# An adapter, attention and quantised feed-forward block on one core: new step orders in the head loop, a fourth mask laid by ScalarE, and an adapter product in strips

## The chip, the cores and the metric

The kernel runs on one core of one Trainium2 chip. The metric is the device time of a launch in microseconds (us). The engines of the core work from their own instruction queues and meet at semaphores: TensorE (PE, with its weight loads as PEld), VectorE (DVE), ScalarE (ACT), GpSimd (POOL) and SyncE (SP), which here only issues transfers.

## What is computed

Eight sequences of 128 tokens with 512 features go through three stages, and each stage adds to x:

```python
h   = x @ W.T + b + 2 * (x @ A[id]) @ B[id]        # rank 16 adapter, one per sequence
q,k,v = dequant_matmul(h)                           # int4 weights, scales per 128 inputs: 4 row groups each
q,k = rope(q), rope(k)                              # 32 query heads, 8 key/value heads of 128
ctx = softmax(causal(q @ k.T / sqrt(128))) @ v
x   = x + dequant_matmul(ctx)                       # output product, 4 column groups per head
y   = (x @ B2[id2].T) @ A2[id2].T                   # second rank 16 adapter
y   = fake_quant_linear(layernorm(y), w1) ; gelu ; fake_quant_linear(y, w3)
out = x + y
```

Each of the 1,024 tokens meets only its own sequence in the attention. The weights w1 and w3 are rounded to 8 bits by row before use.

## The kernel before

All tokens stay in SBUF, features on partitions: `accT` holds x, and `h_hi` and `h_lo` hold the adapter's output as two fp32r parts whose sum is the fp32 value. The program has three parts: a prologue (adapter, weights of the feed-forward, first projections), a head loop of 8 groups (one key/value head and four query heads h = 0 to 3 each, the first and last group written out, six in a hardware loop), and the second adapter with the feed-forward as the tail.

**A step** is one `double_step` of TensorE (L1301, L1302): a 128x128 weight block against all 1,024 tokens of the upper and the lower part, four matmuls of 512 columns into a pair of PSUM banks. There are steps Q 0 to 3 (of a later head's query), K and V 0 to 3 (the next group's key and value, spread over the heads) and O 0 to 3 (the output product). A group has 40 steps. The table `PERIOD` gives their order, and since the three PSUM pairs are taken in turn, a step can start when the one three before it has been drained. ScalarE drains the steps Q0, K0 and V0 with their scale (L728); VectorE drains the others by a multiply and add into `raw_q`, `raw_k`, `raw_v` (L1018) or `accT` (L1032).

**Between the steps** each head has four kinds of fp32 block, in two halves f of four sequences that live in the PSUM banks `flow0` and `flow1`: `turn_probs` (L1410, transposes), `context` (L1418), `scores_ahead` (L1290, the next head's scores), and in head 3 `values_ahead` (L1295, transposes of the next group's v). A half's way through a head is: scores; `maxima` on VectorE (L983); `exps` on ScalarE (L685); `inverse` on VectorE (L1005); `normalise` on GpSimd (L538); `turn_probs`; `keep_turned` on ScalarE (L734); `context`; `keep_upper_context` on ScalarE (L751); `split_context` on VectorE (L1039). The causal mask of the scores is laid into the bank beforehand: by ScalarE (`seed_mask`, L746) for the scores that heads 0 to 2 make, and by a bf16 matmul of 512 columns (L1287) for those that head 3 makes.

**The rotation** of q and k needs each half of the head's 128 rows in the other's place. SyncE copies `raw_q` to `swap_q` by DMA (L408) once Q3 is drained, and `raw_k` to `swap_k` once K3 is. GpSimd then makes cosine part, sine part and sum in two halves each (L507, L519 for q; L523, L527, L533 for k).

**The prologue**: the adapter's first product (`lora_rows`, L1205) is made with the adapters of all eight sequences side by side for all tokens, a mask keeps each token's own 16 rows, and the second product (`linear_lora`, L1247) adds to the linear layer's bank (`linear`, L1242) with a contraction of 128. VectorE rounds the feed-forward weights (`quantise_weights`, L898 to L904). The first K and Q projections are made by halves of the tokens (`early_project`), and head 0 of the first group starts after `scores(1, 0)` and the transposes of v.

Every order is written out by hand in `body` for each engine; nothing is scheduled by a planner. A wait holds everything behind it on its engine.

## Time and profile before

| | us |
|---|---|
| median of 3 runs | 579.5 (579.35, 579.5, 583.7) |
| the profiled execution, its own time | 580.44 |
| its span, first to last instruction | 578.5 |
| granted TensorE clock over the span | 0.999 of full |

```profile
PE 549.6 (95%) x3065; PEld 429.3 (74%) x3069; DVE 494.2 (85%) x643; ACT 353.5 (61%) x923; POOL 399.9 (69%) x410
```

The row gives each engine's busy time, its share of the span and its instructions. The end of a matmul is modelled and contains its way through the array, so that one matmul's time overlaps the next one's: how fast TensorE goes is read from the distance between starts. A fp32 matmul stands in the trace as two instructions.

### The profile page before, as it was taken

What the parts mean: (1) busy time and instruction counts of PE and PEld (TensorE: products, weight loads), DVE (VectorE), ACT (ScalarE), POOL (GpSimd) and SP (SyncE); (2) the same over time, 40 slices, a digit from 0 to 9 for tenths busy, and PEclk for the clock granted to TensorE, in tenths of its full rate; (3) what the DMA queues carried; (4) which work ended last, traced back from release to release, by engine and by line L of the source; (5) the groups of instructions that cost most, each with busy time, mean ns of one, the idle gap of its engine ahead of it and who ended that gap; (6) DMA issues with size and microseconds to landing.
All of it is one profiled execution on the core that took longest, in us unless ns stands there. A gap on an engine that the chain in (4) does not pass through costs nothing.

```text
span 578.5 us, 10344 instructions
## 1 busy us (share of the span) xinstructions
PE 549.6 (95%) x3065; PEld 429.3 (74%) x3069; DVE 494.2 (85%) x643; ACT 353.5 (61%) x923; POOL 399.9 (69%) x410
## 2 busy tenths in 40 slices
PE   5999979999999999999999999999999999987885
PEld 4555557887888888878887888888878887875442
DVE  2894457998999899989998999899989998987897
ACT  2052447666766675666666766676666656765895
POOL 3003186699779977997799779977997799852064
...
GB/s 271 250 97 35 33 151 126 116 69 57 128 127 57 55 127 127 54 54 127 127 54 54 127 127 54 54 127 127 54 54 127 91 54 56 73 19 1 1 19 127
DMA packets 38171, 51.91 MB, mean 90 GB/s; under 512 B 12100, under 2 KB 20452, under 8 KB 38148
## 3 DMA queue, kind: packets, MB, share of 16 engines
...
q14 instruction: 12, 0.10, 0.1%
...
## 4 chain that ended last, share of the span: by engine, by line
PE 80%; DVE 10%; issue 3%; DMA 2%; ACT 2%; POOL 2%; SPq 0%; DVEq 0%; POOLq 0%; ACTq 0%
PE pair L1301 23%; PE pair L1302 22%; PE flow L1290 9%; PE flow L1418 8%; PE flow L1410 4%; PE pair L1242 4%; DVE y_max L1125 2%; DVE raw_v L1018 1%; PE flow L1295 1%; PE pair L1205 1%; PE flow L1242 1%; DVE raw_q L1018 1%; PE pair L1247 1%; DMA raw_q<-in_L_cond_W 1%; DVE rope_c L1137 1%
## 5 line engine op out<-in xcount | busy, mean ns | idle before, releaser
L1032 DVE SCALAR_TENSOR_TENSOR accT<-pair,so_now,accT 128x1024 f32<-128x1024 f32 x125 | 157.6, 1278 | 13.7 <-PE pair L1302 13.0
L1018 DVE SCALAR_TENSOR_TENSOR raw_q<-pair,sc_now,raw_q 128x1024 f32<-128x1024 f32 x90 | 115.5, 1283 | 3.5
L538 POOL TENSOR_TENSOR probs<-probs,rowinv 128x512 f32<-128x512 f32 x64 | 66.7, 1042 | 65.1 <-DVE rowinv L1005 65.0
L1301 PE MATMUL pair<-ctx_hi,wo 128*128 128x512 f32 x256 | 104.8, 409 | 2.7 <-issue 1.5
L685 ACT ACTIVATE probs<-flow,negmax 128x128 f32<-128x128 f32 x248 | 88.0, 370 | 31.0 <-DVE negmax L983 30.9
L1301 PE MATMUL pair<-h_hi,wq 128*128 128x512 f32 x240 | 100.0, 417 | 1.8 <-ACT raw_q L728 1.8
L1302 PE MATMUL pair<-ctx_lo,wo 128*128 128x512 f32 x256 | 100.2, 391 | 0.0
L1302 PE MATMUL pair<-h_lo,wq 128*128 128x512 f32 x240 | 94.1, 392 | 0.0
L507 POOL TENSOR_TENSOR rope_s<-swap_q,consts 128x512 f32<-128x512 f32 x62 | 80.1, 1291 | 10.2 <-DMA swap_q<-raw_q 10.2
L519 POOL TENSOR_TENSOR qT<-rope_c,rope_s 128x512 f32<-128x512 f32 x62 | 79.3, 1280 | 4.4
L507 POOL TENSOR_TENSOR rope_c<-raw_q,consts 128x512 f32<-128x512 f32 x62 | 78.7, 1290 | 0.0
L751 ACT ACTIVATE ctx_hi<-flow 128x512 fp32r<-128x512 f32 x64 | 38.4, 600 | 61.5 <-PE flow L1418 61.5
L1418 PEld LDWEIGHTS flow<-probsT,v_now 128*128 128x128 f32 x512 | 62.2, 191 | 13.7 <-ACT probsT L734 8.7
L1418 PE MATMUL flow<-probsT,v_now 128*128 128x128 f32 x512 | 69.9, 281 | 0.6 <-ACT probsT L734 0.4
L1290 PEld LDWEIGHTS flow<-kT,qT 128*128 128x128 f32 x496 | 65.0, 191 | 5.4 <-ACT flow L746 1.4
L1290 PE MATMUL flow<-kT,qT 128*128 128x128 f32 x496 | 65.4, 275 | 1.2 <-ACT flow L746 1.2
L1301 PEld LDWEIGHTS pair<-ctx_hi,wo 128*128 128x128 f32 x256 | 48.2, 188 | 13.5 <-DVE accT L1032 2.9
L1302 PEld LDWEIGHTS pair<-ctx_lo,wo 128*128 128x128 f32 x256 | 48.2, 188 | 8.5
L1301 PEld LDWEIGHTS pair<-h_hi,wq 128*128 128x128 f32 x240 | 45.2, 188 | 11.9 <-DVE accT L1032 2.2
L685 ACT ACTIVATION_READ_ACCUMULATOR probs<-flow,negmax 128x1 f32 x248 | 51.9, 209 | 0.0
L1039 DVE TENSOR_TENSOR ctx_lo<-flow,ctx_hi 128x512 fp32r<-128x512 f32 x64 | 43.8, 685 | 9.3 <-ACT ctx_hi L751 9.1
L1302 PEld LDWEIGHTS pair<-h_lo,wq 128*128 128x128 f32 x240 | 45.3, 189 | 7.2
...
## 6 DMA issues: line engine op xcount, KB each, us to landing
...
```

Source lines behind the costliest of these rows:

```text
L507: pool.tensor_tensor(per_seq(into[:, f, :]), per_seq(source[:, f, :]), on_each_seq(table), ALU.mult).then_inc(done, 1)
L519: pool.tensor_tensor(qT[:, (h + 1) % 2, half[f]], rope_c[:, f, :], rope_s[:, f, :], ALU.add).then_inc(q_roped, 1)
L538: pool.tensor_tensor(pr, pr, rowinv[:, f, :].unsqueeze(2).broadcast_to([P, HB, P]), ALU.mult).then_inc(probs_done, 1)
L685: e = act.activation(probs[:, 0, f, seq(b)], bank[:, seq(b)], ACT.Exp, bias=negmax[:, f, b:b + 1], accum_out=rowsum[:, f, b:b + 1])
L751: act.activation(ctx_hi[:, h % 2, half[f]], flow[f][:, :], ACT.Copy).then_inc(ctx_kept, 1)
L1018: dve.scalar_tensor_tensor(out=into, in0=flat(pair[pair_of(h, (kind, j), last)][:, :, :]), scalar=sc_now[:, scale_slot(kind, h), j:j + 1], ...
L1032: dve.scalar_tensor_tensor(out=a, in0=flat(pair[pair_of(h, (O, c), last)][:, :, :]), scalar=so_now[:, (h if c == 0 else h - 1) % 2, c:c + ...
L1039: dve.tensor_tensor(ctx_lo[:, h % 2, half[f]], flow[f][:, :], ctx_hi[:, h % 2, half[f]], ALU.subtract).then_inc(ctx_split, 1)
L1290: mm = pe.matmul(bank[:, seq(b)], qT[:, par, t], kT[:, t], start=False, stop=(b == HB - 1), skip_group_check=masked)
L1301: pe.matmul(into[:, f, :], w, upper[:, half[f]], start=True, stop=False)
L1302: mm = pe.matmul(into[:, f, :], w, lower[:, half[f]], start=False, stop=True)
L1418: mm = pe.matmul(flow[f][:, seq(b)], v_now[:, HB * f + b, :], probsT[:, f, seq(b)], start=(b == 0), stop=(b == HB - 1), skip_group_check=True)
```

## The change

It touches the prologue and the loop; the tail from the second adapter on is the same.

**The adapter in strips.** The rows of the adapters are placed so that a strip of 32 partitions holds those of sequences q and q + 4. The first product is 16 matmuls, each with 32 columns of weights and the 256 tokens of its two sequences, to 32 partitions of one bank; one mask by parity follows. The second product is 32 matmuls with a contraction of 32 rows and 128 tokens, in eight rounds of four; each round waits for the one before it.

```diff
-            def lora_rows(f):
+            def lora_rows():
 
                 for c in range(C):
-                    mm = pe.matmul(banks[4 + f], lA[:, c, :], accT[:, c, half[f]], start=(c == 0), stop=(c == C - 1))
-                mm.then_inc(u_done, 1)
+                    tokens = accT[:, c, :].rearrange("p (j b n) -> p b j n", j=2, b=HB)
+                    for q in range(HB):
+                        mm = pe.matmul(banks[4][STRIPS[q], 0:2 * P].rearrange("p (j n) -> p j n", j=2), lA[:, c, STRIPS[q]],
+                                       tokens[:, q, :, :], start=(c == 0), stop=(c == C - 1), skip_group_check=True)
+                        if c == C - 1:
+                            mm.then_inc(u_done, 1)
 
             for o in range(C):
                 turn_x(o, banks[o])
@@ -1239,12 +1506,17 @@
 
                 f, o = k // C, k % C
                 for c in range(C):
-                    pe.matmul(linear_bank(k), WT[:, c, seq(o)], accT[:, c, half[f]], start=(c == 0), stop=False)
-
-            def linear_lora(k):
-                f, o = k // C, k % C
-                pe.wait_ge(u_kept, f + 1)
-                pe.matmul(linear_bank(k), lB[:, seq(o)], uT[:, half[f]], start=False, stop=True).then_inc(lin_done, 1)
+                    pe.matmul(linear_bank(k), WT[:, c, seq(o)], accT[:, c, half[f]], start=(c == 0), stop=(c == C - 1))
+
+            def linear_lora(f):
+                pe.wait_ge(u_kept, 1)
+                for s in range(HB):
+                    wait(pe, strips_done, C * (HB * f + s))
+                    for o in range(C):
+                        q = (o + s) % HB
+                        mm = pe.matmul(linear_bank(C * f + o)[:, seq(q)], lB[STRIPS[q], seq(o)], uT[STRIPS[q], seq(f)],
+                                       start=False, stop=True, skip_group_check=True)
+                        mm.then_inc(strips_done, 1)
```

**Order of the prologue.** The second half of the linear layer is joined, ScalarE takes over two of VectorE's six passes over the feed-forward weights, GpSimd rotates in another order, and the first exponentials `exps(0, 0)` come ahead of the loop.

```diff
             pe.wait_ge(d_la, 16 * 2 * B)
-            lora_rows(0)
+            lora_rows()
             pe.wait_ge(scT_kept, 4)
             turn_weights(2)
-            lora_rows(1)
-            turn_weights(4)
-            for k in range(C):
-                linear_lora(k)
-            turn_weights(6)
+            linear_lora(0)
...
             linear(4)
-            linear_lora(4)
+            linear(5)
             pe.wait_ge(lo_made, C)
             pe.wait_ge(wk_made, 1)
             early_project(K, 0, 0)
-            linear(5)
-            linear_lora(5)
+            turn_weights(4)
+            turn_weights(6)
             pe.wait_ge(wq_made, 1)
             early_project(Q, 1, 0)
             pe.wait_ge(ffT_kept, 4)
             linear(6)
-            linear_lora(6)
             linear(7)
-            linear_lora(7)
+            linear_lora(1)
+            early_project(K, 2, 1)
+            early_project(Q, 3, 1)
             pe.wait_ge(diag_made, 2 * C)
-            pe.wait_ge(lo_made, C + 2)
             for m in range(2):
                 pe.matmul(banks[4 + m], ones, diag[:, m, :], start=True, stop=True).then_inc(ffrow_done, 1)
-            pe.wait_ge(lo_made, 2 * C)
-            early_project(K, 2, 1)
-            early_project(Q, 3, 1)
             pe.wait_ge(k_roped, 1)
             pe.wait_ge(q_roped, 1)
             scores(0, 0, score_bank(0, False))
...
+            def round_weights(k):
+                m, c = k // C, k % C
+                act.wait_ge(ff_top, k + 1)
+                act.activation(w_nat[k], w_nat[k], ACT.Identity, bias=magic, scale=ff_inv[:, m, c:c + 1]).then_inc(ff_rounded, 1)
+
+            def take_weights(k):
+                act.wait_ge(ff_clipped, k + 1)
+                act.activation(w_rounded[k], w_nat[k], ACT.Copy, bias=-HALF_MAGIC).then_inc(ffq_made, 1)
...
             early_wide(V, 5, V_PAIRS[0])
+            exps(0, 0, score_bank(0, False))
```

**The loop.** `PERIOD` and the bodies of all engines have new orders. SyncE issues the weight loads of a head ahead of the swaps, except for the output weights, which come behind. ScalarE lays the mask for the scores of head 3 too (`SEEDED`), the second half of it at the start of the next head 0.

```diff
-        PERIOD = [[(Q, 0), (O, 1), (Q, 1), (Q, 2), (Q, 3), (K, 0), (O, 2), (O, 3), (K, 1), (O, 0)],
-                  [(Q, 0), (O, 1), (Q, 1), (Q, 2), (Q, 3), (K, 2), (O, 2), (O, 3), (K, 3), (O, 0)],
-                  [(Q, 0), (O, 1), (Q, 1), (Q, 2), (Q, 3), (V, 0), (V, 1), (O, 2), (O, 3), (V, 2), (O, 0)],
-                  [(Q, 0), (O, 1), (Q, 1), (Q, 2), (Q, 3), (V, 3), (O, 2), (O, 3), (O, 0)]]
+        PERIOD = [[(Q, 0), (O, 1), (Q, 1), (Q, 2), (K, 0), (Q, 3), (O, 2), (K, 1), (O, 3), (O, 0)],
+                  [(Q, 0), (O, 1), (Q, 1), (Q, 2), (K, 2), (O, 2), (Q, 3), (O, 3), (K, 3), (O, 0)],
+                  [(Q, 0), (O, 1), (V, 0), (Q, 1), (Q, 2), (V, 1), (O, 2), (Q, 3), (O, 3), (V, 2), (O, 0)],
+                  [(Q, 0), (O, 1), (Q, 1), (V, 3), (Q, 2), (Q, 3), (O, 2), (O, 3), (O, 0)]]
...
-        SEEDED = REP - 1
+        SEEDED = REP
...
-                    if h < 2 or not last:
-                        load_output(g + h // 2, (h + 2) % REP)
                     if h == 1 and not last:
                         load_q(g + 1)
+                        if loads:
+                            load_kv(g + 2)
                     if present(h, (Q, 3), first, last):
                         sp.wait_ge(dve_drained, drains_by(g, h, (Q, 3), first, last))
                         wait(sp, q_sin, 2 * n + 2)
                         swap(swap_q, raw_q, swapped_q)
+                    if h < 2 or not last:
+                        load_output(g + h // 2, (h + 2) % REP)
                     if h == 1 and not last:
-                        if loads:
...
+                    elif h == 2:
+                        q_cosine(0)
+                        q_cosine(1)
+                        q_sine(0)
+                        q_add(0)
+                        normalise(0)
+                        k_cosine(0)
+                        normalise(1)
+                        q_sine(1)
+                        q_add(1)
+                        k_sine(0)
+                        k_cosine(1)
+                        query_scale()
+                        output_scale()
+                    else:
+                        q_cosine(0)
+                        q_cosine(1)
+                        q_sine(0)
+                        k_sine(1)
+                        normalise(0)
+                        q_sine(1)
+                        normalise(1)
+                        output_scale()
+                        q_add(0)
+                        k_add(0)
+                        q_add(1)
+                        k_add(1)
+                        query_scale()
```

The bodies of head 3 on TensorE and VectorE, as they are now:

```diff
+                    else:
+                        project(Q, 0)
+                        output(1)
+                        project(Q, 1)
                         project(V, 3)
-                    context(1)
...
+                        turn_probs(0)
+                        project(Q, 2)
+                        context(0)
+                        turn_probs(1)
+                        project(Q, 3)
+                        context(1)
+                        values_ahead(0)
                         output(2)
...
                         output(3)
...
+                        scores_ahead(0)
+                        values_ahead(1)
+                        output(0)
                         scores_ahead(1)
```

ScalarE's mask, and the start of head 0:

```diff
+                        if h == 3:
+                            act.wait_ge(v_kept, 2 * (g + 1) + f + 1)
+                        else:
+                            act.wait_ge(ctx_split, 2 * n + f + 1)
                         act.activation(per_seq(flow[f][:, :]), on_each_seq(tri), ACT.Copy).then_inc(mask_seeded, 1)
...
+                    def seed_mask_before():
+
+                        if not first and SEEDED == REP:
+                            act.wait_ge(v_kept, 2 * g + 2)
+                            act.activation(per_seq(flow[1][:, :]), on_each_seq(tri), ACT.Copy).then_inc(mask_seeded, 1)
...
+                    elif h == 0:
+                        round_kv()
+                        round_output()
+                        round_query()
+                        keep_values_before()
+                        seed_mask_before()
+                        exps_now(0)
+                        drain_query()
+                        exps_now(1)
```

Three places in the order of the instructions. First TensorE in the prologue, from the last part of the first half's linear layer to the first K projection. Before:

```order
L1242 MATMUL pair<-accT,WT 128x512 x12
L1218 MATMUL flow<-consts,rope_c 128x128
L1221 MATMUL flow<-consts,rope_c 128x32 x2
L1225 MATMUL flow<-consts,rope_c 128x32 x4
L1235 MATMUL flow<-ident_b,w_q 128x128 x8
L1205 MATMUL pair<-accT,qT 128x512 x4
L1235 MATMUL flow<-ident_b,w_q 128x128 x8
L1205 MATMUL pair<-accT,qT 128x512 x4
L1235 MATMUL flow<-ident_b,y_qT 128x128 x8
L1247 MATMUL pair<-kT,qT 128x512 x4
L1235 MATMUL flow<-ident_b,y_qT 128x128 x8
L1242 MATMUL pair<-accT,WT 128x512 x4
```

And now (L1509 is the linear layer, L1502 the transposes of rounded weights, L1470 and L1517 the two products of the adapter):

```order
L1509 MATMUL pair<-accT,WT 128x512 x12
L1485 MATMUL flow<-consts,rope_c 128x128
L1488 MATMUL flow<-consts,rope_c 128x32 x2
L1492 MATMUL flow<-consts,rope_c 128x32 x4
L1502 MATMUL flow<-ident_b,w_q 128x128 x8
L1470 MATMUL pair<-accT,qT 32x256 x16
L1502 MATMUL flow<-ident_b,w_q 128x128 x8
L1517 MATMUL pair<-raw_v,qT 128x128 x16
L1509 MATMUL pair<-accT,WT 128x512 x8
```

Eight matmuls of the first product became 16 of a quarter of the size each way, the second product of the first half is one block of 16, and two blocks of transposes moved behind the first K projection.

Second, ScalarE from the end of head 3 to the first exponentials of head 0, in the hardware loop, whose first instruction is the branch. Before:

```order
L751 ACTIVATE ctx_hi<-flow 128x512
L739 ACTIVATE v_now<-flow 128x512
L319 UNCONDITIONAL_BRANCH
L319 ISA
L755 ISA
L660 ACTIVATE wo<-wo_i 128x512
L668 ISA
L660 ACTIVATE wq<-wq_i 128x512
L738 REGISTER_ALU
L739 ACTIVATE v_now<-flow 128x512
L683 ISA
L685 ACTIVATE probs,rowsum<-flow,negmax 128x128 x4
```

And now (L849 and L860 lay the mask, L747 turns integer weights into fp32r):

```order
L839 ACTIVATE v_now<-flow 128x512
L849 ACTIVATE flow<-consts 128x512
L326 UNCONDITIONAL_BRANCH
L326 ISA
L747 ACTIVATE wkv<-wkv_i 128x512
L868 ISA
L870 ISA
L747 ACTIVATE wo<-wo_i 128x512
L755 ISA
L747 ACTIVATE wq<-wq_i 128x512
L838 REGISTER_ALU
L839 ACTIVATE v_now<-flow 128x512
```

The mask of flow0 is laid behind the copy of the first half's values; ahead of the copy of the second half's stands one more conversion of weights, and behind it the second mask.

Third, GpSimd in head 2 of the hardware loop, from the first cosine on. Before (L507 cosine and sine of q, L538 normalise, L519 sum of q, L523 and L527 cosine and sine of k):

```order
L507 TENSOR_TENSOR rope_s<-swap_q,consts 128x512
L538 TENSOR_TENSOR probs<-probs,rowinv 128x512 x2
L551 REGISTER_ALU
L552 ISA
L552 COPY so_now<-so_cols 128x4
L519 TENSOR_TENSOR qT<-rope_c,rope_s 128x512
L507 TENSOR_TENSOR rope_s<-swap_q,consts 128x512
L519 TENSOR_TENSOR qT<-rope_c,rope_s 128x512
L522 ISA
L523 TENSOR_TENSOR raw_k<-raw_k,consts 128x512
L527 TENSOR_TENSOR swap_k<-swap_k,consts 128x512
L523 TENSOR_TENSOR raw_k<-raw_k,consts 128x512
```

And now (L521, L552, L533, L537 and L541 in the same roles):

```order
L521 TENSOR_TENSOR rope_s<-swap_q,consts 128x512
L533 TENSOR_TENSOR qT<-rope_c,rope_s 128x512
L552 TENSOR_TENSOR probs<-probs,rowinv 128x512
L536 ISA
L537 TENSOR_TENSOR raw_k<-raw_k,consts 128x512
L552 TENSOR_TENSOR probs<-probs,rowinv 128x512
L521 TENSOR_TENSOR rope_s<-swap_q,consts 128x512
L533 TENSOR_TENSOR qT<-rope_c,rope_s 128x512
L541 TENSOR_TENSOR swap_k<-swap_k,consts 128x512
L537 TENSOR_TENSOR raw_k<-raw_k,consts 128x512
```

The first sum of q moved ahead of the first normalise, and the first cosine of k, with its wait for the DMA of `swap_k`, between the two normalises.

## Rows read from the trace of the kernel before

**Rows 1.** The page: shares of the chain that ended last, by engine.
```profile
PE 80%; DVE 10%; issue 3%; DMA 2%; ACT 2%; POOL 2%; SPq 0%; DVEq 0%; POOLq 0%; ACTq 0%
```
**Rows 2.** Stretches (start:end length), busy PE PEld DVE ACT POOL: first head; heads of group 2.
```profile
82.53:97.37 14.84, 11.86 (x71) 9.43 (x70) 7.61 (x10) 12.65 (x38) 11.35 (x12) 1.00 0.29 72
197.82:211.70 13.88, 13.88 (x84) 11.76 (x82) 11.59 (x14) 9.57 (x26) 12.27 (x13) 1.00 0.26 63
211.70:225.40 13.70, 13.70 (x83) 11.76 (x82) 13.34 (x16) 8.63 (x25) 9.86 (x10) 1.00 0.52 147
225.40:240.14 14.74, 14.74 (x88) 12.51 (x86) 14.21 (x16) 10.12 (x30) 11.32 (x13) 1.00 0.44 107
240.14:254.88 14.74, 14.41 (x89) 11.78 (x88) 13.71 (x16) 9.03 (x28) 13.73 (x15) 1.00 0.22 53
```
**Rows 3.** Timeline of TensorE: start, duration, line, operation, count [idle before <-releaser].
```profile
196.78 0.39 PE L1287 MATMUL flow<-tri_b,ident_b 128*128 128x512 bf16 x1
197.01 1.05 PE L1290 MATMUL flow<-kT,qT 128*128 128x128 f32 x8
...
201.59 0.60 PE L1410 MATMUL flow<-consts,probs 128*128 128x128 f32 x4
201.95 0.48 PE L1301 MATMUL pair<-h_hi,wq 128*128 128x512 f32 x1
202.26 0.39 PE L1302 MATMUL pair<-h_lo,wq 128*128 128x512 f32 x1
202.49 0.40 PE L1301 MATMUL pair<-h_hi,wq 128*128 128x512 f32 x1
...
233.89 1.05 PE L1418 MATMUL flow<-probsT,v_now 128*128 128x128 f32 x8
234.70 0.48 PE L1301 MATMUL pair<-ctx_hi,wo 128*128 128x512 f32 x1
...
249.90 0.66 PE L1295 MATMUL flow<-consts,raw_v 128*128 128x128 f32 x4 [0.33 <-DVE raw_v L1018]
```
**Rows 4.** Timeline of VectorE, group 3: two adds to accT, three drains of one Q.
```profile
264.85 2.47 DVE L1032 SCALAR_TENSOR_TENSOR accT<-pair,so_now,accT 128x1024 f32<-128x1024 f32 x2
...
272.75 3.92 DVE L1018 SCALAR_TENSOR_TENSOR raw_q<-pair,sc_now,raw_q 128x1024 f32<-128x1024 f32 x3
```
**Rows 5.** Timeline of ScalarE, group 3: one mask laid into a flow bank.
```profile
264.11 0.60 ACT L746 ACTIVATE flow<-consts 128x512 f32<-128x512 f32 x1
```
**Rows 6.** The tile swap_k in groups 1 to 6: its DMA.
```profile
DMA to landing us min/median/max: 3.3/3.6/4.0
```
**Rows 7.** Timeline of GpSimd, group 2: the first normalise of head 2.
```profile
228.08 1.04 POOL L538 TENSOR_TENSOR probs<-probs,rowinv 128x512 f32<-128x512 f32 x1 [2.64 <-DVE rowinv L1005]
```
**Rows 8.** Timeline of TensorE: adapter products whole, and the tail's product in strips.
```profile
29.41 3.65 PE L1205 MATMUL pair<-accT,qT 128*128 128x512 f32 x8
...
37.28 3.65 PE L1247 MATMUL pair<-kT,qT 128*128 128x512 f32 x8
...
531.55 1.78 PE L1501 MATMUL flow<-accT,low_bT 128*32 128x256 f32 x24
```
**Rows 9.** Timeline, end of the prologue: second K half, its swap, the scores.
```profile
65.38 2.46 DVE L967 SCALAR_TENSOR_TENSOR raw_k<-pair,sc_now,raw_k 128x512 f32<-128x512 f32 x3 [1.58 <-ACT raw_k L674]
...
72.59 1.29 POOL L476 TENSOR_TENSOR raw_k<-raw_k,consts 128x512 f32<-128x512 f32 x1 [11.33 <-DMA swap_k<-raw_k]
...
80.47 0.38 PE L1287 MATMUL flow<-tri_b,ident_b 128*128 128x512 bf16 x1 [1.41 <-POOL qT L481]
```
**Rows 10.** Timeline, head 0 of the first group: TensorE's longest wait.
```profile
86.45 0.50 PE L1301 MATMUL pair<-h_hi,wq 128*128 128x512 f32 x1 [1.75 <-ACT raw_q L728]
```
**Rows 11.** Timeline, last group: the last swap of q, and the scores it leads to.
```profile
503.83 1.10 SPq L408 DMA_DIRECT2D swap_q<-raw_q  x2
...
508.78 1.29 POOL L507 TENSOR_TENSOR rope_s<-swap_q,consts 128x512 f32<-128x512 f32 x1 [1.28 <-DMA swap_q<-raw_q]
...
517.20 1.05 PE L1290 MATMUL pair<-kT,qT 128*128 128x128 f32 x8
```

587 lines of the change are left out of this document (406 added, 181 removed).

## The prediction

> **What bounds the kernel now.** I read the shares of the chain first: TensorE holds 80% of it [rows 1], so a gain must come out of TensorE's own time or out of its waits. Then the stretches by head: the four heads of a loop group take 13.88 + 13.70 + 14.74 + 14.74 = 57.06 us, TensorE is called busy for nearly all of it, and VectorE for 11.59 + 13.34 + 14.21 + 13.71 = 52.85 [rows 2]. Busy does not tell how full TensorE is, so the timeline comes next, by distances between starts [rows 3]. A matmul of 512 columns follows another after 0.23 us (202.26 to 202.49), 0.91 to 0.92 for a step of four. The first one behind an fp32 block takes 0.31 (201.95 to 202.26), 0.08 more. A `turn_probs` takes 0.36 (201.59 to 201.95), a `context` 0.81 (233.89 to 234.70); scores have the same eight instructions of 1.05 us and I take 0.81; a mask matmul takes 0.23 (196.78 to 197.01).
>
> A group is then 40 steps x 0.91 = 36.4, 8 x (0.36 + 0.81 + 0.81) = 15.8, two value transposes 0.7 and two mask matmuls 0.5, together 53.4. It has 21 places where an fp32 block ends and a step follows: 21 x 0.08 = 1.7. That makes 55.1 of 57.06: 1.9 us of a group are waits, the largest the value transposes behind VectorE's last drain of v (0.33 alone [rows 3]). VectorE has 4.2 us of room in a group.
>
> **The loop, part by part.** *Fewer block ends.* The new order sets blocks side by side (both turns in head 0, both contexts in heads 0 and 2, both scores in heads 0 to 2). I count 15 ends instead of 21: 6 x 0.08 = 0.5 us less. *Fourth mask by ScalarE.* Two mask matmuls go, 0.5 us; ScalarE lays two more masks at 0.60 [rows 5] and is busy 9.57 + 8.63 + 10.12 + 9.03 = 37.35 of 57 us in those heads [rows 2], so the work fits; its place is the question, below. *VectorE's order.* Adds to accT follow each other after 1.19 (2.47 less a last one of 1.28), the three drains of one Q after 1.32 (3.92 less 1.28, halved), since each waits for its predecessor's result [rows 4]. The new order separates five of eight such neighbours: 5 x 0.13 = 0.6 us less. The ideal sums are now TensorE 54.1 and VectorE 52.2.
>
> *New and kept waits.* I laid the four heads out with these durations, starting TensorE's step as soon as its pair is drained and each engine in its written order. Head 0: the second turn waits for exponentials 1 and normalise 1, 0.3. Head 1: context 1 waits for ScalarE's copy, 0.1. Head 2: V1 and context 1 wait for ScalarE, 0.3 together. Head 3: context 0 and 1, 0.3, and scores 1: ScalarE must copy the second half's values (after three conversions of weights) and only then lay the mask, about 0.6 + 0.6 behind the end of the transposes, against 1.0 for the O0 step between them, so 0.5. With rounding of starts that makes 1.7 us, the group 55.8, and I take **1.2 us less a group**. The bounds: all waits gone, 57.06 - 54.1 = 2.9 less; none of it gained, 0. I take a value nearer to the waits of the layout, since VectorE stands in it without a pause in heads 1 and 2 and passes on every delay. Six groups of the hardware loop: -7.2. Heads 1 to 3 of the first group: -0.9.
>
> *SyncE's order.* The query and key/value loads now go ahead of head 1's swap of q, and stand well before it; the output loads go behind it, two heads ahead of their use. A swap of k takes 3.3 to 4.0 us to land [rows 6]. K3's drain moves later, to about 0.4 us into head 2, so it lands at about 4.2. Behind it GpSimd now holds the second normalise of head 2, which must end by 7.9, when TensorE turns it: cosine 1.3 and normalise 1.0 make it 6.5. Nothing, but see the rivals. GpSimd used to idle 2.64 us ahead of head 2's first normalise [rows 7]; the sum of q now fills that.
>
> **The prologue.** Each adapter product takes 3.49 us for a half (3.65 less the tail of the last [rows 8]), 14.0 in all. In strips: the tail's product of the same shape issues 24 instructions in 1.78, so 8 in about 0.5 to 0.6 [rows 8]; the first product has 32, 2.2 us instead of 7.0. The second has 64 of half the columns in eight rounds of 8, and each round waits for the last to end: at least the issue of a round and one latency, 0.5 to 0.6 a round, 4.4 instead of 7.0. TensorE loses 7.4 us of work. Not all reaches the loop: the split of the second half into upper and lower part used to lie beside the linear steps and now comes behind all of it (passes of 128x512 on ScalarE and VectorE in turn, about 0.6 each as the mask in [rows 5]: I let the first projection of that half start 1.5 us behind the last strip). Followed on, the drain of the second K half ends at 61 to 62 instead of 67.84 [rows 9], its swap lands 4.7 us later as before (67.84 to 72.59 [rows 9]), GpSimd has made both cosines in that time, so the scores that waited until 80.47 for its sum could start at 71 to 72; TensorE's and VectorE's own queue of wide Q and V steps comes to them at 73 to 74 and ends some 6 us earlier than before. **-5.8**, bounds: -2 if strips and split eat the rest, -8 if TensorE's queue has no waits of its own.
>
> The Trainium skill ("TensorE: Matmul & The Clock Gate", the cost: per-tile semaphore tail) says that increments of concurrent tiles' semaphores serialize, 25 + 4.7 ns a tile + 26.3 ns an increment. By that, eight rounds of four increments would cost 8 x 0.15 = 1.2 us more than nothing, an estimate from that page; the tail's strips above have an increment on each matmul and their 1.78 contains it.
>
> **First head.** It took 14.84 us [rows 2]; its seven steps and blocks need 7 x 0.91 + 4.0 + 0.4 = 10.8. The largest wait is 1.75 for ScalarE, which made the first exponentials before it drained Q0 [rows 10]. Those are now made beside the wide steps. A wait on the second half's exponentials stays (about 1.1), and the two contexts, whose copies feed the masks, stay in line. I take 12.9: **-2.0**, bounds 0 and -3.5.
>
> **Last group.** Its head 2 is short and waits for head 3's query: swap issued at 503.83, landed 508.78, scores 517.20 [rows 11]. Q3 now stands behind both turns and a context in head 1 (0.36 + 1.0 + 0.81 + 0.36 = 2.5 us later on TensorE; VectorE, then behind two more operations, ends it some 1.4 later). Heads 0 and 1 give back 0.2. **+1.2**, bounds -0.5 and +3.
>
> **Sum.** -5.8 - 2.0 - 0.9 - 7.2 + 1.2 = -14.7 on the profiled execution's 580.44: 565.7. The median of the runs shown is 579.5, 0.9 below it: **565**.
>
> **Rivals.**
> 1. *VectorE sets the pace of the loop, or its lag turns into waits at S1 and the masks, and a group stays at 56.6 or more.* For: 52.2 of work in a group, no pause in two heads. Against: it had 4.2 us of pauses before, nearly all ahead of steps, which the new order fills. With a group as before (0 for -8.1) 573; at 56.6, 570. Chance 0.17.
> 2. *The waits nearly all go.* For: the orders fit each other, and my layout rounds up. Groups of 54.6: -2.4 x 6.7, first part as forecast: 557; with all bounds 553. Chance 0.22.
> 3. *The strips give nothing*: the rounds' waits and the late split take back the whole 5.8. For: eight waits of the engine on itself. Against: the tail's row. 571. Chance 0.07.
> 4. *Slower.* GpSimd's second normalise in head 2 is queued behind the wait for `swap_k`. If the copy lands later than 5.5 us into head 2, TensorE waits at its second turn, 1 us for 1 us, in seven groups. To lose the 14.7 us it must be late by 2.1 more, at 7.6; landing at 8.7 (twice the usual time) gives 3.2 x 7 = 22, 565 + 22 = 587. Against: no swap of k in the loop took more than 4.0 [rows 6], and the loads that could crowd it are now issued before it. Chance 0.03.
> 5. *The change does not do what it says*: the mask by ScalarE is the one part that could cost more than it saves (0.5 for 0.5 a group); then 568. It lies in the forecast's range. Chance of the forecast itself, 558 to 569: 0.51.
>
> **Numbers.** About 1% (6 us) is what a measurement of this kernel can tell from no change. Range 554 to 573: it leaves out rival 4, the worse half of rival 1 and the best of rival 2. Faster than 573.7: forecast 0.51, rival 2 0.22, rival 3 0.06, rival 1 0.10, together 0.89. Same 0.08, slower 0.03.
>
> **What would show it.** First instruction of the head loop (it was 82.53) at 76 to 77, a first head of 13; a loop group of 55.8 instead of 57.06, with TensorE's waits in head 3 named after ScalarE's mask; VectorE at 52 in a group; in the last group some 1.4 us more from the end of head 0 to the last head's scores. Wrong would be: a loop group that waits for DMA of `swap_k`, VectorE without pauses and TensorE waiting for drains of pairs, or strips whose four matmuls don't overlap.

## The result

| | before | changed | forecast |
|---|---|---|---|
| median | 579.4 (4 runs, 579.07 to 583.7) | 574.4 (4 runs, 573.36 to 576.33) | 565, range 554 to 573 |
| ratio to before | | 0.990, interval 0.987 to 0.993 | 0.975 |
| profiled execution | 580.44, span 578.5 | 574.92, span 573.1 | |

The change made the kernel 5 us faster, a third of what was forecast, and the time lies outside the range. Cut at the starts of the same steps, the two spans compare so (us; a group ends where the first step behind the second scores of its head 3 starts). Head 0 of the first group is taken with the same seven steps in both kernels, which in the changed one means up to the end of O0, since O0 there stands behind the second scores:

| stretch | before | changed | difference | forecast |
|---|---|---|---|---|
| up to the head loop | 82.53 | 77.88 | -4.65 | -5.8 |
| head 0 of the first group, seven steps | 14.84 | 13.10 | -1.74 | -2.0 |
| heads 1 to 3 of it | 43.36 | 42.85 | -0.51 | -0.9 |
| six groups of the hardware loop | 342.50 | 342.04 | -0.46 | -7.2 |
| last group | 48.32 | 50.30 | +1.98 | +1.2 |
| tail | 46.95 | 46.93 | -0.02 | 0 |

The first two rows together brought 6.4 us of the 7.8 that were forecast. The hole is in the loop: 8.1 us were expected of its six groups and of the three heads ahead of them, and 1.0 came. The first row is not exact: in the fourteen traces with the new prologue (this one and the experiments) the loop starts between 76.7 and 78.9, 77.6 on average, and of the kernel before there is one trace.

### The profile page after: what moved, and what is told of

Its sections match the earlier page's. It is cut to its first block, busy times and chain, and to the rows that moved or that the text cites. A ratio compares the mean times of both kernels' runs of the same rounds, so it can differ in the third digit from the quotient of the medians.

```text
span 573.1 us, 10488 instructions
## 1 busy us (share of the span) xinstructions
PE 540.5 (94%) x3115; PEld 426.1 (74%) x3119; DVE 484.9 (85%) x626; ACT 369.3 (64%) x953; POOL 399.7 (70%) x410
## 4 chain that ended last, share of the span: by engine, by line
PE 72%; DVE 10%; issue 6%; POOL 5%; DMA 4%; ACT 3%; ACTq 0%; SPq 0%; DVEq 0%; POOLq 0%
PE pair L1572 20%; PE pair L1573 20%; PE flow L1686 9%; PE flow L1561 9%; PE flow L1678 4%; PE pair L1509 4%; DMA swap_q<-raw_q 2%; DVE y_max L1388 2%; POOL probs L552 1%; DMA stage<-in_x 1%; PE flow L1509 1%; POOL rope_s L521 1%; PE flow L1698 1%; DVE accT L1230 1%; DVE raw_q L1216 1%
## 5 line engine op out<-in xcount | busy, mean ns | idle before, releaser
L1572 PE MATMUL pair<-ctx_hi,wo 128*128 128x512 f32 x256 | 106.2, 415 | 3.8 <-DVE accT L1230 1.7
L552 POOL TENSOR_TENSOR probs<-probs,rowinv 128x512 f32<-128x512 f32 x64 | 66.7, 1042 | 54.4 <-DVE rowinv L1203 54.2
L1572 PE MATMUL pair<-h_hi,wq 128*128 128x512 f32 x240 | 98.0, 408 | 0.3 <-ACT raw_q L828 0.3
L521 POOL TENSOR_TENSOR rope_s<-swap_q,consts 128x512 f32<-128x512 f32 x62 | 80.1, 1293 | 22.2 <-DMA swap_q<-raw_q 22.2
L533 POOL TENSOR_TENSOR qT<-rope_c,rope_s 128x512 f32<-128x512 f32 x62 | 79.8, 1288 | 4.4
L521 POOL TENSOR_TENSOR rope_c<-raw_q,consts 128x512 f32<-128x512 f32 x62 | 78.5, 1289 | 3.6 <-DVE raw_q L1216 2.0
L834 ACT ACTIVATE probsT<-flow 128x512 f32<-128x512 f32 x64 | 37.4, 597 | 51.9 <-PE flow L1678 51.9
L1561 PEld LDWEIGHTS flow<-kT,qT 128*128 128x128 f32 x496 | 60.5, 191 | 11.1 <-issue 6.3
L1686 PE MATMUL flow<-probsT,v_now 128*128 128x128 f32 x512 | 66.9, 279 | 0.3 <-ACT probsT L834 0.2
L1561 PE MATMUL flow<-kT,qT 128*128 128x128 f32 x496 | 62.5, 276 | 4.3 <-ACT flow L860 3.8
```

The costliest lines, as they stand in the source:

```text
L521: pool.tensor_tensor(per_seq(into[:, f, :]), per_seq(source[:, f, :]), on_each_seq(table), ALU.mult).then_inc(done, 1)
L533: pool.tensor_tensor(qT[:, (h + 1) % 2, half[f]], rope_c[:, f, :], rope_s[:, f, :], ALU.add).then_inc(q_roped, 1)
L552: pool.tensor_tensor(pr, pr, rowinv[:, f, :].unsqueeze(2).broadcast_to([P, HB, P]), ALU.mult).then_inc(probs_done, 1)
L1561: mm = pe.matmul(bank[:, seq(b)], qT[:, par, t], kT[:, t], start=False, stop=(b == HB - 1), skip_group_check=masked)
L1572: pe.matmul(into[:, f, :], w, upper[:, half[f]], start=True, stop=False)
L1686: mm = pe.matmul(flow[f][:, seq(b)], v_now[:, HB * f + b, :], probsT[:, f, seq(b)], start=(b == 0), stop=(b == HB - 1), skip_group_check=True)
```

## The profile after

The page of the changed kernel, shares of the engines and of the chain that ended last (before: [rows 1]):

```profile
PE 540.5 (94%) x3115; PEld 426.1 (74%) x3119; DVE 484.9 (85%) x626; ACT 369.3 (64%) x953; POOL 399.7 (70%) x410
PE 72%; DVE 10%; issue 6%; POOL 5%; DMA 4%; ACT 3%; ACTq 0%; SPq 0%; DVEq 0%; POOLq 0%
```

TensorE still holds the chain, but GpSimd has 5% of it where it had 2%.

Stretches of the changed kernel, as in [rows 2]: the first head, up to its second scores and with O0 behind them, and the four heads of one group. The heads end behind their second scores. Since O0 now follows these in heads 0 and 1, head 0 has a step less here than in [rows 2] and head 2 one more; with the same steps as there, heads 0, 1 and 2 take 13.78, 13.74 and 14.76:

```profile
77.88:89.96 12.08, 10.82 (x68) 8.67 (x66) 6.94 (x8) 9.96 (x22) 9.60 (x11) 1.00 0.20 46
77.88:90.98 13.10, 11.84 (x72) 9.51 (x70) 7.10 (x8) 10.86 (x27) 9.80 (x11) 1.00 0.25 61
191.53:204.30 12.77, 12.77 (x79) 11.07 (x78) 10.61 (x14) 8.33 (x20) 9.24 (x13) 1.00 0.25 62
204.30:218.05 13.75, 13.75 (x84) 11.73 (x82) 13.50 (x17) 8.98 (x26) 9.81 (x10) 1.00 0.46 135
218.05:233.81 15.76, 15.76 (x91) 13.26 (x90) 15.08 (x18) 9.67 (x26) 13.54 (x14) 1.00 0.45 115
233.81:248.38 14.57, 14.01 (x88) 11.66 (x86) 13.52 (x16) 11.33 (x35) 14.56 (x15) 1.00 0.22 54
```

The group is 56.85 long where it was 57.06. VectorE (third pair of numbers) is busy for 52.71 where it was 52.85: the 0.6 us that the new order of its adds and drains was to save is 0.14. And the last row shows GpSimd (fifth pair) busy for 14.56 of 14.57 us in head 3, without a pause, where [rows 2] have 13.73 of 14.74.

The end of that head 3 on TensorE (start, duration, line; in brackets the idle time ahead and what ended it):

```profile
244.49 1.05 PE L1561 MATMUL flow<-kT,qT 128*128 128x128 f32 x8
245.37 0.60 PE L1698 MATMUL flow<-consts,raw_v 128*128 128x128 f32 x4
245.73 0.48 PE L1572 MATMUL pair<-ctx_hi,wo 128*128 128x512 f32 x1
...
246.51 0.39 PE L1573 MATMUL pair<-ctx_lo,wo 128*128 128x512 f32 x1
247.47 1.15 PE L1561 MATMUL flow<-kT,qT 128*128 128x128 f32 x8 [0.56 <-ACT flow L860]
```

and ScalarE beside it:

```profile
245.22 0.62 ACT L747 ACTIVATE wq<-wq_i 128x512 fp32r<-128x512 int32 x1
246.01 0.60 ACT L839 ACTIVATE v_now<-flow 128x512 f32<-128x512 f32 x1 [0.17 <-PE flow L1698]
246.64 0.60 ACT L860 ACTIVATE flow<-consts 128x512 f32<-128x512 f32 x1
```

From 246.51 to 247.47 are 0.96 us where a matmul of a step takes 0.23: 0.73 of waiting in every group. The scores themselves then take 1.15 where those at 244.49 take 1.05, since their second instruction comes late too, so 0.8 in all. ScalarE's three conversions are done before it is due (it idles 0.17 for the transposes); what takes the time is the chain: from the end of the transposes (245.73) 0.28 to the copy, 0.60 for it, 0.03, 0.60 for the mask and 0.23 to the scores, 1.74 with one step of 1.0 beside it. The two mask matmuls that this replaced took 0.46.

Where two fp32 blocks now stand side by side: both scores of head 1 in group 2, with the second half's row once more by itself, and both turns of head 0 in group 3.

```profile
216.35 1.95 PE L1561 MATMUL flow<-kT,qT 128*128 128x128 f32 x16
...
217.24 1.06 PE L1561 MATMUL flow<-kT,qT 128*128 128x128 f32 x8
218.05 0.48 PE L1572 MATMUL pair<-ctx_hi,wo 128*128 128x512 f32 x1
218.36 0.40 PE L1573 MATMUL pair<-ctx_lo,wo 128*128 128x512 f32 x1
...
253.10 1.04 PE L1678 MATMUL flow<-consts,probs 128*128 128x128 f32 x8
253.89 0.48 PE L1572 MATMUL pair<-h_hi,wq 128*128 128x512 f32 x1
```

Both scores take 1.70, where twice 0.81 is 1.62; both turns 0.79, where twice 0.36 is 0.72. The first half of the scores takes 0.89, eight times 0.11, and the second, with a step behind it, 0.81. Behind that, the step's second matmul comes 0.31 after its first instead of 0.23. So the 0.08 of the forecast is no price of a block's end: the step starts 0.03 behind the block's last instruction, and its second matmul makes up for it (0.03 + 0.31 = 0.11 + 0.23). It is due behind every half of a block, whatever follows, and setting blocks side by side saves nothing.

By the starts of single instructions, in groups 2 to 6 of either kernel, an fp32 instruction of a transpose is followed after 0.109 us, one of contexts or scores after 0.112, and a matmul of a step or a mask after 0.23 (medians). A group has 40 instructions of the first kind, 128 of the second and 160 matmuls of steps: 4.4 + 14.3 + 36.8 = 55.5 us, and 0.23 for each mask matmul. What a group is longer than that are waits and pauses:

| us in a group | length | by count | waits and pauses |
|---|---|---|---|
| before | 57.08 | 55.96 | 1.1 |
| changed | 56.85 | 55.50 | 1.4 |
| e1, old loop | 57.05 | 55.96 | 1.1 |
| e2, two masks by TensorE | 56.54 | 55.96 | 0.6 |
| e3, one mask by TensorE | 56.31 | 55.73 | 0.6 |
| e4, transposes earlier | 57.00 | 55.50 | 1.5 |
| e10, e4 with VectorE's adds | 56.32 | 55.50 | 0.8 |
| e6, blocks set apart | 58.83 | 55.50 | 3.3 |

Of the 1.1 before, 0.5 is the transposes of v behind VectorE's drain ([rows 3] show the row); of the 1.4 now, 0.8 is the mask and 0.2 the first turn of head 3 behind GpSimd's normalise. The rest are pauses of 0.02 to 0.1, most of them inside the contexts, whose cause no run shows. So the old group had 1.1 us of waits where the forecast had 1.9, and the new one is 0.46 shorter by count, by the masks alone, where the forecast had 1.0.

## The experiments

All times are medians, and the ratio is against the kernel before in the same batch, whose median was 579.4 to 581.1; so ratios compare better than times. A group is the median of groups 2 to 6 of the loop in the trace, and "last" the last group up to the tail.

| run | median | ratio, interval | group | last |
|---|---|---|---|---|
| the changed kernel | 574.4 | 0.990 (0.987-0.993) | 56.85 | 50.30 |
| e1 old loop | 574.5 | 0.990 (0.988-0.993) | 57.05 | 48.33 |
| e2 mask by TensorE | 572.7 | 0.986 (0.983-0.989) | 56.54 | |
| e3 half the mask | 571.4 | 0.986 (0.983-0.988) | 56.31 | 50.3 |
| e4 transposes earlier | 575.8 | 0.992 (0.990-0.994) | 57.0 | |
| e5 head 1 old | 579.1 | 0.998 (0.997-1.000) | 57.68 | 49.52 |
| e6 blocks apart | 588.5 | 1.013 (1.010-1.017) | 58.83 | 50.97 |
| e7 exponentials in head 0 | 575.9 | 0.993 (0.990-0.996) | 56.85 | |
| e8 one wait | 577.3 (1 run) | | 56.86 | 50.8 |
| e9 e3, last group old | 569.9 | 0.982 (0.980-0.985) | 56.28 | 48.35 |
| e10 e4, VectorE's adds | 571.5 | 0.985 (0.983-0.987) | 56.32 | 50.3 |
| e11 GpSimd old in head 2 | 579.1 | 0.998 (0.996-1.000) | 57.43 | |
| e12 SyncE old | 578.5 | 0.997 (0.996-0.999) | 57.37 (56.9 to 57.7) | |
| e13 e10, last group old | 569.5 | 0.980 (0.977-0.983) | 56.34 | |

### Is the loop's new order worth anything?

**e1.** All four engines' bodies, `PERIOD`, the masks and SyncE's order of the loop as before, the new prologue kept:

```diff
-        SEEDED = REP
+        SEEDED = REP - 1
...
-        PERIOD = [[(Q, 0), (O, 1), (Q, 1), (Q, 2), (K, 0), (Q, 3), (O, 2), (K, 1), (O, 3), (O, 0)],
+        PERIOD = [[(Q, 0), (O, 1), (Q, 1), (Q, 2), (Q, 3), (K, 0), (O, 2), (O, 3), (K, 1), (O, 0)],
...
```

> The changed kernel's start (strips, order of the prologue, first exponentials ahead of the loop) with the loop and the last group in the old orders, three masks a group by ScalarE and the old order of SyncE's issues. Theory A (the start brought 7.4 us, the loop about nothing, the last group lost 2.0): loop from 77.9 on, a first head of about 13.0, heads 1 to 3 of the first group 43.4, groups 57.05, a last group of 48.3; span 572, time 573.5 to 574 against 574.4 of the changed kernel. Rival B (the new loop orders are worth 1 us a group, and something in the new start takes it away from the groups behind it): groups of 57.05 still, but first group or last group longer by some us, time 578 or more.

Groups of 57.05 and a last group of 48.33 came as theory A had them, and a first head of 13.42, 0.4 above it; rival B, with its 578 us or more, is out. The median, 574.5, is no better than the changed kernel's 574.4, and the start of the loop scatters by 2 us, so the stretch behind it tells more: 495.94 us before, 494.22 in e1, 495.22 in the changed kernel. The gain of 5 us comes from the new prologue alone, with the first exponentials in it. The new orders of loop and last group together cost 1.0: they win 0.8 in the first group (0.3 of it in head 0, 13.10 against 13.42 with the same seven steps) and 0.2 in the six groups, and lose 2.0 in the last.

### The mask

**e2, e3.** Both masks of head 3 by TensorE again, or that of the second half alone:

```diff
-        SEEDED = REP
+        SEEDED = REP - 1
...
-                            pe.wait_ge(mask_seeded, 2 * SEEDED * g + 2 * h + f + 1)
+                            pe.wait_ge(v_kept, 2 * g + 2 + f + 1)
```

```diff
-                        if not first and SEEDED == REP:
+                        if False:
                             act.wait_ge(v_kept, 2 * g + 2)
...
                         if h == 3:
-                            pe.wait_ge(mask_seeded, 2 * SEEDED * g + 2 * h + f + 1)
+                            if f == 0:
+                                pe.wait_ge(mask_seeded, 7 * g + 7)
+                            else:
+                                pe.wait_ge(v_kept, 2 * g + 4)
...
-                        scores(f, (h + 1) % 2, score_bank(f, last and h == 2), seeded(h, last))
+                        scores(f, (h + 1) % 2, score_bank(f, last and h == 2), seeded(h, last) and not (h == 3 and f == 1))
```

> The changed kernel with head 3's two masks laid by TensorE's bf16 matmuls again and nothing else. Theory A (the second mask in head 3 is what TensorE waits 0.73 us for, and two mask matmuls cost 0.46): groups of 56.6 instead of 56.85, time 572.5. Rival B (VectorE sets the pace of the groups, the wait only shows its lag): the wait moves elsewhere and the matmuls come on top, groups of 57.3, time 577. Rival C (no difference): 574.4.

> The changed kernel with the mask of head 3's first half by ScalarE as now, and that of the second half by a bf16 matmul of TensorE. Theory A: the wait of 0.73 goes, 0.23 comes, groups of 56.35, time 571.4. Rival B (VectorE sets the pace): 56.85 to 57.1, time 574.4 to 576.

572.7 and 571.4, groups of 56.54 and 56.31: theory A in both, to 0.1 us a group. The place in e3, where no matmul waits:

```profile
301.67 0.39 PE L1573 MATMUL pair<-ctx_lo,wo 128*128 128x512 f32 x1
301.90 0.39 PE L1558 MATMUL flow<-tri_b,ident_b 128*128 128x512 bf16 x1
302.12 1.05 PE L1561 MATMUL flow<-kT,qT 128*128 128x128 f32 x8
302.93 0.48 PE L1572 MATMUL pair<-h_hi,wq 128*128 128x512 f32 x1
```

So the second mask by ScalarE cost 0.8 to save 0.23, and since the wait's removal goes straight into the time, VectorE does not set the pace of a group of 56.85.

**e4, e10.** The other way: keep the mask with ScalarE, but make the transposes early enough (TensorE's part of the edit; ScalarE's copy and mask of the second half move from the next head 0 to the end of head 3).

```diff
                         values_ahead(0)
                         output(2)
+                        values_ahead(1)
                         output(3)
                         scores_ahead(0)
-                        values_ahead(1)
                         output(0)
```

> The changed kernel with the transposes of the second half's values two steps earlier in head 3 (between steps O2 and O3), and ScalarE's copy and mask of it in head 3 too, so that two steps and the first scores lie between the transposes and the scores that need the mask. Theory A: the wait before the second scores of 0.73 goes, one of up to 0.3 for VectorE's split comes before the transposes, groups of 56.3 to 56.4, time 571 to 571.5. Rival B (VectorE sets the pace): 56.8, time 574.4.

575.8: neither. The wait for the mask did go, but another came. VectorE in e4:

```profile
304.25 0.69 DVE L1184 TENSOR_REDUCE negmax<-flow 128x4 f32<-128x512 f32 x1 [1.16 <-PE flow L1562]
304.86 2.47 DVE L1231 SCALAR_TENSOR_TENSOR accT<-pair,so_now,accT 128x1024 f32<-128x1024 f32 x2
```

and TensorE:

```profile
307.38 0.50 PE L1573 MATMUL pair<-ctx_hi,wo 128*128 128x512 f32 x1 [0.44 <-DVE accT L1231]
```

VectorE's next operation is the maximum of scores that are now 0.36 later; it idles 1.16 with the adds of O3 and O0 queued behind, and TensorE then awaits the pair they hold. e10 lets it add O3 first:

```diff
                         add_output(2)
-                        maxima_ahead(0)
                         add_output(3)
+                        maxima_ahead(0)
                         add_output(0)
```

> e4_v1_early (groups of 57.0, VectorE idle 1.15 us ahead of a maximum with an add behind it that TensorE's next step awaits) with VectorE adding O3 ahead of that maximum in head 3. Theory A (the order of VectorE ate what the earlier transposes had won): groups of 56.2 to 56.5, time 571 to 571.8. Rival B (the first scores, 0.36 us later than in the changed kernel, are what costs): 56.9, time 575.

571.5, groups of 56.32. VectorE's idle time there is 0.35, ahead of the add:

```profile
300.14 1.28 DVE L1231 SCALAR_TENSOR_TENSOR accT<-pair,so_now,accT 128x1024 f32<-128x1024 f32 x1 [0.35 <-PE pair L1574]
301.35 0.68 DVE L1184 TENSOR_REDUCE negmax<-flow 128x4 f32<-128x512 f32 x1
```

### Blocks apart and side by side

**e6.** The blocks of head 0 set apart:

```diff
                         turn_probs(0)
-                        turn_probs(1)
                         project(Q, 3)
+                        turn_probs(1)
+                        output(2)
                         context(0)
+                        project(K, 1)
                         context(1)
-                        output(2)
-                        project(K, 1)
                         output(3)
                         scores_ahead(0)
-                        scores_ahead(1)
                         output(0)
+                        scores_ahead(1)
```

> The changed kernel with the fp32 blocks of head 0 set apart again on TensorE: a step between the two transposes of probabilities, one between the two contexts, one between the two scores, the steps themselves in the same order. Theory A (0.08 us come with each half's block, beside another block or not): the sum of the small pitches in head 0 the same, groups of 56.85 within 0.15 plus what new waits show by name. Rival B (0.08 only where a block ends and a step follows, as the forecast had it): three more such places, 0.24 a group more, 57.1, 1.7 us in all.

Groups of 58.83: theory A, with its new waits, which came to far more than it looked for. Setting the blocks apart has no price of its own. The distances of the single instructions are those of the changed kernel (0.109, 0.112 and 0.23, a step 0.03 behind a block's last instruction), so that rival B's 0.24 is not there, and the 1.98 more are waits: about 1.3 in head 0, of them 0.5 for ScalarE's mask and 0.44 for VectorE's adds, and the rest behind it, most of it while VectorE is late. Why contexts should stand together is seen on VectorE:

```profile
262.89 0.69 DVE L1237 TENSOR_TENSOR ctx_lo<-flow,ctx_hi 128x512 fp32r<-128x512 f32 x1 [1.47 <-ACT ctx_hi L854]
264.86 0.69 DVE L1237 TENSOR_TENSOR ctx_lo<-flow,ctx_hi 128x512 fp32r<-128x512 f32 x1 [1.28 <-ACT ctx_hi L854]
```

It idles 2.75 us for two splits; its room in a group is 56.85 - 52.71 = 4.1, and from 264.86 to 281.25 it never pauses again.

**e8.** A single run, 577.3, of use for its trace. The waits of both halves ahead of the first scores:

> The changed kernel, in head 0 of each group the waits of both halves' scores set ahead of the first half's. Theory A (the 0.08 us that two adjacent halves take beyond 2 x 0.81 is the wait between them): sixteen instructions of scores in 1.62 instead of 1.70. Rival B (it comes with the bank or the first matmul of a half): 1.70.

```profile
261.40 1.95 PE L1561 MATMUL flow<-kT,qT 128*128 128x128 f32 x16
263.10 0.48 PE L1572 MATMUL pair<-ctx_hi,wo 128*128 128x512 f32 x1
```

1.70 again, rival B: it is not the wait between the halves. Nor is it the bank: the first instruction of the second half comes 0.11 behind the last one of the first, as every other one in these sixteen. The 1.62 was the wrong measure, as shown above.

**e13.** e10 with the last group of e9:

> e10_v1_early_dve (both masks of head 3 by ScalarE, the second half's transposes two steps earlier, VectorE's adds ahead of the maximum; 571.5, groups of 56.3) with heads 0 and 1 of the last group in the old order, as in e9 (569.9, one mask in head 3 by TensorE, groups of 56.3). Theory A (without its waits a group is 56.0 to 56.3 long, whichever way the wait for the mask is taken away, since what is left are the 27 small pitches behind the halves of fp32 blocks): groups of 56.2 to 56.4, time 569.3 to 570. Rival B (waits are left that the forecast's sum of 54.1 has no room for, and the two ways add up, 0.46 us of mask matmuls among them): groups of 55.9 or less, time 567.5 or less.

569.5, groups of 56.34: theory A by its numbers, but not for its reason, and that the two ways end at the same length is in part luck. By count e13 has 55.5 and 0.8 of waits and pauses (0.2 for a split of the context ahead of the transposes, 0.2 at the first turn of head 3), e3 has 55.7, with its mask matmul, and 0.6. A group's own length on TensorE is 55.5 us with all masks laid by ScalarE, not 54.1.

### The last group

**e5, e9.** e5 puts head 1 of every group back, e9 heads 0 and 1 of the last group only (on e3):

```diff
+        ENDING = [[(Q, 0), (O, 1), (Q, 1), (Q, 2), (Q, 3), (K, 0), (O, 2), (O, 3), (K, 1), (O, 0)],
+                  [(Q, 0), (O, 1), (Q, 1), (Q, 2), (Q, 3), (K, 2), (O, 2), (O, 3), (K, 3), (O, 0)]] + PERIOD[2:]
...
+                    if last and h < 2:
+                        project(Q, 0)
...
+                        project(Q, 3)
+                        turn_probs(0)
+                        turn_probs(1)
+                        context(0)
+                        context(1)
```

> The changed kernel with head 1 of every group in the old order on TensorE and VectorE (Q3 ahead of the contexts, K2 between them), so that the last group's third query is drained early again. Theory A (the last group's 2.0 us are Q3's new place: normalise of the second half, the drain of Q3 and the swap behind it): last group 48.5 to 48.8 instead of 50.3, groups of the loop 56.8 to 57.0, time 572.7 to 573. Rival B (they come from head 0 of the last group, whose second normalise TensorE awaits 0.8 us, and from waits on pairs in the short heads): last group 49.8 or more, time 574.

> e3_mask_half (571.4, groups of 56.35, last group 50.35) with heads 0 and 1 of the last group alone in the old order on TensorE, VectorE and ScalarE; the loop keeps the new one. Theory A (in the last group, where no K and V steps are, the new order costs 2.0: 1.45 in heads 0 and 1 by waits that a K step would cover, 0.6 in head 2 by the later query): last group 48.3, time 569.4. Rival B (half of it comes with the state that the loop leaves, as in e5, where only 0.8 came back): last group 49.5, time 570.6.

e9, shown here by TensorE's part (VectorE and ScalarE likewise), gives the old 48.35 back and 569.9. In the changed kernel TensorE waits in the short heads 0 and 1, where a K step stands in the other groups (first two rows), and the last head's scores wait for its query (last row):

```profile
481.06 0.66 PE L1678 MATMUL flow<-consts,probs 128*128 128x128 f32 x4 [0.83 <-POOL probs L552]
...
494.07 0.50 PE L1572 MATMUL pair<-ctx_hi,wo 128*128 128x512 f32 x1 [0.58 <-DVE raw_q L1216]
...
511.65 0.38 PE L1558 MATMUL pair<-tri_b,ident_b 128*128 128x512 bf16 x1 [0.23 <-POOL qT L533]
```

The swap of that query and what waits for it:

```profile
498.88 1.10 SPq L415 DMA_DIRECT2D swap_q<-raw_q  x2
...
503.38 1.28 POOL L521 TENSOR_TENSOR rope_s<-swap_q,consts 128x512 f32<-128x512 f32 x1 [1.63 <-DMA swap_q<-raw_q]
```

The swap is issued 23.0 us into the group (before: 20.6, [rows 11]) and in use at 27.5 (25.6), and the last head's scores, which wait for the query in the kernel before too, come 2.0 later. That is the whole loss of the group. TensorE itself loses 1.5 in heads 0 and 1 and 0.5 in head 2; the waits in the first two rows are part of what makes the query late.

e5 missed its theory A: the last group fell only to 49.52, and the loop's groups rose to 57.68. Its K3 is made behind the first scores again, but GpSimd's new head 2 asks for `swap_k` between its normalises. Its waits in the loop (waiter, releaser: us, times, longest):

```profile
POOL raw_k L537 <- DMA swap_k<-raw_k: 8.6, 6, 1.5
```

### GpSimd and SyncE

**e11** puts GpSimd's head 2 back to both normalises first, with the cosine of k behind both sums of q, **e12** SyncE's order of issues:

```diff
+                        normalise(0)
+                        normalise(1)
+                        output_scale()
                         q_add(0)
-                        normalise(0)
-                        k_cosine(0)
-                        normalise(1)
                         q_sine(1)
                         q_add(1)
+                        k_cosine(0)
                         k_sine(0)
                         k_cosine(1)
                         query_scale()
-                        output_scale()
```

```diff
                     n = REP * g + h
+                    if h < 2 or not last:
+                        load_output(g + h // 2, (h + 2) % REP)
                     if h == 1 and not last:
                         load_q(g + 1)
-                        if loads:
-                            load_kv(g + 2)
...
-                    if h < 2 or not last:
-                        load_output(g + h // 2, (h + 2) % REP)
                     if h == 1 and not last:
+                        if loads:
+                            load_kv(g + 2)
```

> The changed kernel with GpSimd's old order in head 2 (both normalises ahead of the sum of q and of the cosine of k). Theory A (the sum of q ahead of the first normalise makes TensorE's turns wait for a late swap of q, which costs 0.9 us in the loop's first group and 0.1 in the others): first loop group 56.9 instead of 57.7, the others 56.7 to 56.85, time 573 to 573.5. Rival B (head 2's order on GpSimd costs nothing, the first group is slow for another reason): 574.4, or slower, when q's sum then comes late for the scores.

> The changed kernel with SyncE's issues in the old order (output weights first, then the query weights, then the swap of q, then the key and value weights). Theory A (the new order of issues is worth nothing, as the forecast had it): 574.4, first loop group 57.7. Rival B (the 1 MB of query weights and the key and value weights delay the swap of q in heads 1 and 2 of the loop's first group): the first group 56.9, time 573.5. Rival C (the new order is what keeps GpSimd's waits short): some groups longer, 576.

Both theories A were wrong, by 6 and 4 us; rival C of e12 had the kind of it, longer groups, but 2.5 us too few (the first loop group is 58.7, against its rival B). TensorE in e11, head 3, and the same place in e12:

```profile
297.21 0.66 PE L1678 MATMUL flow<-consts,probs 128*128 128x128 f32 x4 [0.58 <-POOL probs L552]
```

```profile
296.15 0.66 PE L1678 MATMUL flow<-consts,probs 128*128 128x128 f32 x4 [0.68 <-POOL probs L552]
```

and GpSimd in e12, head 2:

```profile
282.38 1.30 POOL L537 TENSOR_TENSOR raw_k<-raw_k,consts 128x512 f32<-128x512 f32 x1 [0.88 <-DMA swap_k<-raw_k]
```

Behind these places GpSimd works to the end of head 3 without a pause; what it idled there (0.62 for the second `rowinv` in e11, 0.88 for the copy of k in e12) TensorE waits for at the first turn of head 3. In e12 `swap_k` takes 3.3 to 5.3 us to land in the loop, with the key and value loads issued 2 us ahead of it; in the changed kernel 3.1 to 3.8, and in the kernel before, with these loads 4.5 us ahead, 3.3 to 4.0. In e12:

```profile
DMA to landing us min/median/max: 3.3/4.0/5.3
```

So the new orders on GpSimd and SyncE bring nothing over the kernel before, but the new TensorE order needs both.

### The first head

**e7.** `exps(0, 0)` back behind the start of the loop:

```diff
-            exps(0, 0, score_bank(0, False))
...
                     if first and h == 0:
+                        exps_now(0)
                         drain_query()
```

> The changed kernel with the first exponentials made inside head 0 of the first group again, ahead of the drain of Q0. Theory A: head 0 of the first group becomes 1.5 to 2.0 us longer (13.6 to 14.1 instead of 12.1), time 576. Rival B (head 0's gain comes from the new order of its steps and drains): 12.1 to 12.5, time 574.4 to 574.8.

575.9, the head 13.01 instead of 12.08 (both up to the second scores): 0.9, between the two. TensorE's wait for ScalarE's drain of Q0 is 1.21 there and 0.30 in the changed kernel. Of the 1.74 that the head's seven steps won, 0.9 is this and 0.3 the new order (e1); the other 0.5 was not taken apart.

## Why the forecast was wrong

**The step that failed** is the loop group: "53.4 + 1.7 = 55.1 of 57.06: 1.9 us of a group are waits", and "6 x 0.08 = 0.5 us less". The sum measured a block by the distance from its start to the next step, which leaves out 0.08 of its last instruction, and gave the 0.08 back only at the 21 places where a block ends and a step follows, not behind all 26 halves of blocks (0.4 short); a step matmul, taken at 0.91 / 4, has a distance of 0.23 (another 0.4). By count the old group is 56.0 and has 1.1 us of waits and pauses instead of 1.9. Of the 1.2 us that a group was to win, the joined blocks, put at 0.5, gave nothing; the masks gave their 0.46; and the waits, which were to fall from 1.9 to 1.7, rose from 1.1 to 1.4. The new group is 55.5 by count, not the "ideal" 54.1.

**The mask** was put down to wait 0.5 and cost nothing on balance. It waits 0.8. The chain of copy and mask was named rightly, but as "0.6 + 0.6" it left out 0.28 from the transposes to the copy and 0.23 from the mask to the scores; the three conversions ahead of it are not in its way. With the 0.46 saved that is a loss of 0.3 a group (e2: 56.54, 0.31 less), 2 us in all; rival 5 had named this part as the one that could cost more than it saves.

**VectorE's 0.6** was 0.14. A saving by distance from the predecessor is only had where the operation behind was already released; here many of them wait for their step or their split (VectorE's idle time ahead of the drains of Q is 7.4 us in the whole changed kernel and was 3.5).

**Rival 1** (a group of 56.6 or more, chance 0.17) names the length that came, but not its cause: VectorE does not set the pace (e2, e3). **Rival 4** (GpSimd's queue behind `swap_k`, 0.03) did not happen in the changed kernel, where GpSimd never waits for that copy in the loop, but e12 and e5 show it at work as soon as the copy comes late. In the first loop group, 57.70 long, TensorE's turns wait for GpSimd's normalise, itself behind a late `swap_q`:

```profile
162.74 1.29 POOL L521 TENSOR_TENSOR rope_s<-swap_q,consts 128x512 f32<-128x512 f32 x1 [2.13 <-DMA swap_q<-raw_q]
```

That this is why the group is longer than the others is not shown: GpSimd idles 1.85 at the same place of group 3, and e11, which was to take it back, left the group at 57.74.

**The prologue** was right in its mechanism and 1.2 us too hopeful by this trace, 0.9 by the average start. The products in strips:

```profile
32.84 0.50 PE L1517 MATMUL pair<-raw_v,qT 32*128 32x128 f32 x8
33.51 0.50 PE L1517 MATMUL pair<-raw_v,qT 32*128 32x128 f32 x8 [0.17 <-PE pair L1517]
```

A round takes 0.67 (forecast 0.5 to 0.6), the first product 1.87 (2.2), all of it some 6.8 us instead of 14.0. By the Trainium skill ("TensorE: Matmul & The Clock Gate", the cost: per-tile semaphore tail) four tiles with four increments have a tail of 25 + 19 + 105 = 149 ns, an estimate from that page; the trace's gap of 0.17 in each round is near it. No run made the rounds with fewer increments, so how much of the gap they are is not shown. The second K half is drained at 62.2, 5.6 earlier, as forecast (61 to 62). What was missed stands behind it on TensorE: the four matmuls of the feed-forward's rows (L1600), which used to run ahead of that projection, now run between it and the wide steps.

```profile
62.82 1.88 PE L1600 MATMUL pair<-probsT,consts 128*128 128x512 f32 x4
...
67.73 1.12 ACT L766 ACTIVATE raw_q<-pair,sc_now 128x1024 f32<-128x1024 f32 x1 [0.36 <-PE pair L1580]
```

The same drain of the first wide step in the kernel before:

```profile
71.67 1.12 ACT L679 ACTIVATE raw_q<-pair,sc_now 128x1024 f32<-128x1024 f32 x1 [0.36 <-PE pair L1309]
```

It comes 3.9 earlier, not 5.6: the four matmuls take 1.7 (62.82 to 64.54). VectorE's six wide drains of Q and V then run as before, at about 1.35 each, but without a pause of 0.7 between the two, and the transposes of v wait for the last of them, so that the loop starts 4.65 earlier. This is read from the two traces; no run moved the four matmuls back.

```profile
77.03 1.09 PE L1566 MATMUL pair<-consts,raw_v 128*128 128x128 f32 x8 [0.80 <-DVE raw_v L1178]
```

**The first head** (-2.0, came -1.74 with its seven steps) and **the last group** (+1.2, came +1.98) had the right sign. In the last group the later query is the mechanism that was forecast, but it comes 2.0 later instead of 1.4, and heads 0 and 1, which I had put at a gain of 0.2, lose 1.5 by waits.
